# Attention block on one Trainium2 core: scores from two float32r parts, two heads in two 64-row tiles, one exponential over two banks

## The reference

```
mod = silu(c) @ wmod                       # sa, ca, ga, sb, cb, gb
h   = layernorm(x) * (1 + ca) + sa
q, k, v = lora_linear(h, ...)              # 16 heads of 16
scores  = q k^T / 4, causal mask, softmax
x   = x + ga * lora_linear(softmax(scores) v, wo, ao, bo)
h   = layernorm(x) * (1 + cb) + sb
x   = x + gb * (top-2-of-4 experts: relu(h Wi^T + lora_e) Wo^T, weighted)
```

## Time and profile before

| | |
|---|---|
| timed runs (3) | median 2151.95 us, 2151.85 to 2155.94 |
| span of the profiled execution | 2145.5 us |
| its own time | no separate one is given; the median of the runs is 6.45 us above its span |
| busy PE / DVE / ACT / POOL | 1892.0 / 1199.8 / 938.8 / 529.7 us |
| granted TensorE clock, mean | 0.959 |

### The profile page before, as it was taken

How to read it: one execution, slowest core, us unless ns; L and a number is a source line. 1 busy time by engine, 2 the same in 40 slices (tenths; PEclk the granted TensorE clock), 3 DMA queues, 4 the chain that set the end, 5 groups by cost and what they waited for, 6 DMA issues and landing times.

```text
span 2145.5 us, 36829 instructions
## 1 busy us (share of the span) xinstructions
PE 1892.0 (88%) x11124; PEld 980.5 (46%) x11124; DVE 1199.8 (56%) x2697; ACT 938.8 (44%) x1701; POOL 529.7 (25%) x823
## 2 busy tenths in 40 slices
PE   8687888999889989899889998899898998798858
PEld 5233343455435454354534555354543545344435
DVE  3755567555665557655575556655576554755132
ACT  2254444544444544544444444444445443544421
POOL 3111122322222212223223222222122232132223
PEclk9889989999999999999999999999999999999979
DMA  5523333121433222232331214332222323210100
GB/s 170 80 50 60 60 57 78 22 63 23 80 60 67 33 39 77 31 70 32 65 79 20 62 24 81 60 67 33 36 70 41 70 31 65 31 26 16 35 0 20
DMA packets 72349, 111.82 MB, mean 52 GB/s; under 512 B 13940, under 2 KB 41680, under 8 KB 72152
## 3 DMA queue, kind: packets, MB, share of 16 engines
q1 hardware_dynamic: 72136, 109.31, 27.3%
q10 hardware_dynamic: 16, 0.02, 0.0%
HBM read 75.20 MB, written 33.57 MB: 51 GB/s over the span
## 4 chain that ended last, share of the span: by engine, by line
PE 61%; DVE 14%; DMA 8%; issue 7%; SPq 5%; ACT 4%; POOL 0%; DVEq 0%; POOLq 0%; ACTq 0%
PE mxs L747 11%; PE ov L776 9%; PE st L761 9%; PE dense L856 8%; DMA k_st<-k_parts_scratch 8%; PE dense L841 5%; DVE negm L1147 4%; PE dense L867 4%; PE dense L791 4%; SPq L577 4%; PE dense L833 3%; PE dense L733 3%; PE mxs L751 2%; SPq L581 1%; DVE stats L1018 1%
## 5 line engine op out<-in xcount | busy, mean ns | idle before, releaser
L915 ACT ACTIVATE probs<-st 128x512 f32<-128x512 f32 (+1 forms) x1216 | 666.9, 576 | 651.2 <-PE st L761 613.2
L747 PE MATMUL mxs<-k_st,q_st 96*128 96x512 bf16 (+3 forms) x1536 | 463.4, 333 | 54.6 <-DMA k_st<-k_parts_scratch 48.2
L1147 DVE TENSOR_REDUCE negm<-mxs 128x1 f32<-128x512 f32 (+4 forms) x736 | 416.1, 613 | 147.8 <-PE mxs L751 147.4
L761 PE MATMUL st<-q_st,k_st 98*128 98x512 bf16 (+3 forms) x1536 | 453.0, 335 | 38.9 <-issue 24.3
L1147 DVE TENSOR_REDUCE negm_left<-mxs 128x1 f32<-128x512 f32 x512 | 330.0, 684 | 168.0 <-PE mxs L747 165.5
L776 PE MATMUL ov<-probs,v_g 128*32 128x512 f32 (+3 forms) x3072 | 333.5, 506 | 22.7 <-POOL probs L634 21.9
L747 PEld LDWEIGHTS mxs<-k_st,q_st 96*128 96x128 bf16 x1536 | 149.0, 98 | 333.9 <-issue 101.7
L856 PE MATMUL dense<-c_t,wi_t 128*128 128x512 f32 x512 | 247.3, 605 | 4.3 <-ACT ratio_b L965 3.7
L631 POOL TENSOR_TENSOR fence<-fence 128x1 f32<-128x1 f32 x256 | 49.9, 195 | 756.8 <-ACT probs L915 756.6
L761 PEld LDWEIGHTS st<-q_st,k_st 98*128 98x128 bf16 x1536 | 140.1, 99 | 202.6 <-issue 76.3
L655 POOL TENSOR_TENSOR hid<-hid,second 128x512 f32<-128x512 f32 x128 | 159.8, 1270 | 245.1 <-DVE second L1211 244.6
(11 more groups left out here) (162 smaller groups left out, 1715.3 us busy)
## 6 DMA issues: line engine op xcount, KB each, us to landing
q_st<-q_parts_scratch SPq DMA_DIRECT2D x192, 128.0 KB, 6.9
k_st<-k_parts_scratch SPq DMA_DIRECT2D x192, 128.0 KB, 7.4
q_parts_scratch<-q_part SPq DMA_DIRECT2D x16, 768.0 KB, 3.3
k_parts_scratch<-k_part SPq DMA_DIRECT2D x16, 768.0 KB, 5.4
xin<-in_L_attn_x SPq DMA_DIRECT2D x9, 1024.0 KB, 5.1
x<-in_L_attn_x SPq DMA_DIRECT2D x8, 1024.0 KB, 10.6
out_x<-ob SPq DMA_DIRECT2D x64, 128.0 KB, 1.7
q_st<-m_row SPq DMA_DIRECT2D x128, 4.0 KB
```

What stands on the lines that cost most here:

```text
L747: last = nc.tensor.matmul(mxs[:, bank_m, j * n:(j + 1) * n], q_st[0:KS, slot, h0 + j, qt * P:(qt + 1) * P], k_st[0:KS, slot, h0 + j, k0:k0 ...
L761: last = nc.tensor.matmul(st[:, score_bank(ch, kt, h0), j * n:(j + 1) * n], k_st[0:KS + 2, slot, h0 + j, kt * P:(kt + 1) * P], q_st[0:KS + ...
L915: nc.scalar.activation(probs[:, par, h0:h0 + heads, 0:n], st[:, score_bank(ch, kt, h0), 0:heads * n].rearrange("p (j q) -> p j q", q=n), A ...
L1147: nc.vector.tensor_reduce(dst[:, h0:h0 + heads], src, axis=AX.X, op=ALU.max, negate=True).then_inc(max_free, 1)
```

## The change

Queries and keys are split in two float32r parts (ACT copies the first, DVE subtracts the second; POOL's part is gone). Three products of parts replace six, so a head needs 48 rows (50 with the maximum), and two heads stand in one stack, at rows 0 and 64. The matmuls of the two heads come in pairs, in two 64-row tiles, into two banks. A `qk` step now fills both banks of `st`, and one exponential reads both; PE waits for the exponential of the step before. An `mx` step fills two of the three `mxs` banks, DVE still reduces bank by bank (42 in a group, 21 steps); the causal mask is one matmul per bank. `q_part` and `k_part` have one buffer for the two halves of the heads. The planner's costs and positions are new: each `qk` step stands at the position of the nearest `mx` step.

```diff
-Q_PARTS = (0, 0, 1, 1, 0, 2)
-K_PARTS = (0, 1, 0, 1, 2, 0)
+Q_PARTS = (0, 0, 1)
+K_PARTS = (0, 1, 0)
+SK = len(Q_PARTS) * DH
+HALF = 64
+STACK_DMAS = 2 * 2 * len(Q_PARTS)
...
+def max_banks():
+    banks = []
     for qt in range(7, -1, -1):
         if qt >= 4:
-            steps += [(h, 1, qt, 0) for h in range(HG)]
-        heads = {0: [4], 1: [2, 2] if qt < 4 else [2, 1, 1]}.get(qt % 4, [1] * HG)
-        steps += [(sum(heads[:i]), n, qt, qt // 4) for i, n in enumerate(heads)]
+            banks += [(h, 1, qt, 0) for h in range(HG)]
+        heads = 2 if qt % 4 == 0 or qt == 5 else 1
+        banks += [(h, heads, qt, qt // 4) for h in range(HG // heads)]
+def max_steps():
+    banks = max_banks()
+    return [(i, banks[i], banks[i + 1]) for i in range(0, len(banks), 2)]
...
-    heads = {128: 4, 256: 2}.get(n, 1)
-    return [("qk", slot, c, kt, h, heads) for h in range(0, HG, heads)]
+    pairs = 2 if unit_queries(c, kt)[1] <= 256 else 1
+    return [("qk", slot, c, kt, p, pairs) for p in range(0, HG // 2, pairs)]
...
-        _, _, _, heads, qt, chunk = step
-        return (max_keys(qt, chunk) + P * (qt // 4 == chunk)) * heads / 2.4
+        _, heads, qt, chunk = step[3]
+        return 200 + (max(max_keys(qt, chunk), 256) + 2 * P * (qt // 4 == chunk)) * heads / 2.4
...
-    unit_cost = [8 * 512 / 2.4 if kt < 4 * c else 8 * (512 - 128 * (kt % 4)) / 2.4 for c, kt in UNITS]
-
-    row_maxima = [0, 3, 4, 4, 5, 5, 6, 6, 6, 0, 0, 0] if post else [0, 4, 4, 5, 6, 6, 5, 5, 4, 0, 0, 0]
+    unit_cost = [500 + (2 * max(n, 256) + 4 * n) / 2.4 for n in (unit_queries(c, kt)[1] for c, kt in UNITS)]
+
+    row_maxima = [0, 2, 2, 2, 3, 3, 3, 3, 3, 0, 0, 0] if post else [0, 2, 2, 3, 3, 3, 3, 3, 2, 0, 0, 0]
...
-        turns = [((i + 0.5) / len(following), 0, s) for i, s in enumerate(following)]
-        turns += [((i + 0.35) / len(mx), 1, s) for i, s in enumerate(mx)]
+        pairs_at = [(i + 0.5) / len(mx) for i in range(len(mx))]
+        turns = [(at, 1, s) for at, s in zip(pairs_at, mx)]
+        for i, s in enumerate(following):
+            at = (i + 0.5) / len(following)
+            turns.append((min(pairs_at, key=lambda t: abs(t - at)) if mx else at, 0, s))
...
-        q_part = sb("q_part", [P, 2, 3, S], BF16)
-        q_st = sb("q_st", [P, 2, HG, S], BF16)
+        q_part = sb("q_part", [P, 2, S], F32R)
+        q_st = sb("q_st", [P, 2, HG // 2, S], F32R)
...
-                    for s in range(SPLIT):
-                        for dst, src, part in ((q_st, q_d, Q_PARTS[s]), (k_st, k_d, K_PARTS[s])):
-                            heads = src[ot, rows, part, :].rearrange("(j d) n -> d j n", j=HG)
-                            sp.dma_start(dst[s * DH:(s + 1) * DH, slot, :, :], heads).then_inc(stack_in[slot], 16)
+                    for s, (qp, kp) in enumerate(zip(Q_PARTS, K_PARTS)):
+                        for half in range(2):
+                            r0 = HALF * half + s * DH
+                            for dst, src, part in ((q_st, q_d, qp), (k_st, k_d, kp)):
+                                heads = src[ot, rows, part, :].rearrange("(p b d) n -> b d p n", p=HG // 2, b=2)
+                                sp.dma_start(dst[r0:r0 + DH, slot, :, :].bitcast(F32),
+                                             heads[half]).then_inc(stack_in[slot], 16)
...
-                elif kind == "pj":
-                    pool.wait_ge(part2_ready, done("pj") + 1)
-                    nc.gpsimd.tensor_tensor(dst[:, 2, :], rest[:, par, :], dst[:, 1, :],
-                                            ALU.subtract).then_inc(part3_ready, 1)
...
+                    after(pe, max_free, 2 * done("mx") - MAX_BANKS + 2)
                     for j in range(heads):
-                        last = nc.tensor.matmul(mxs[:, bank_m, j * n:(j + 1) * n],
-                                                q_st[0:KS, slot, h0 + j, qt * P:(qt + 1) * P],
-                                                k_st[0:KS, slot, h0 + j, k0:k0 + n], start=True, stop=True)
+                        for i in range(2):
+                            rows = slice(HALF * i, HALF * i + SK)
+                            last = nc.tensor.matmul(mxs[:, (first + i) % MAX_BANKS, j * n:(j + 1) * n],
+                                                    q_st[rows, slot, banks[i][0] // 2 + j, qt * P:(qt + 1) * P],
+                                                    k_st[rows, slot, banks[i][0] // 2 + j, k0:k0 + n],
+                                                    start=(j == 0), stop=True, skip_group_check=True)
+                            if not diagonal:
+                                last.then_inc(max_full, 1)
...
-                    after(pe, exp_done, done("qk") - SCORE_BANKS + 1)
-                    for j in range(heads):
-                        last = nc.tensor.matmul(st[:, score_bank(ch, kt, h0), j * n:(j + 1) * n],
-                                                k_st[0:KS + 2, slot, h0 + j, kt * P:(kt + 1) * P],
-                                                q_st[0:KS + 2, slot, h0 + j, q0:q0 + n], start=True, stop=True)
+                    after(pe, exp_done, done("qk"))
+                    for p in range(pairs):
+                        for i in range(2):
+                            rows = slice(HALF * i, HALF * i + SK + 2)
+                            last = nc.tensor.matmul(st[:, i, p * n:(p + 1) * n],
+                                                    k_st[rows, slot, p0 + p, kt * P:(kt + 1) * P],
+                                                    q_st[rows, slot, p0 + p, q0:q0 + n], start=True, stop=True)
...
-                    nc.scalar.activation(probs[:, par, h0:h0 + heads, 0:n],
-                                         st[:, score_bank(ch, kt, h0), 0:heads * n].rearrange("p (j q) -> p j q", q=n),
+                    heads = probs[:, par, 2 * p0:2 * (p0 + pairs), 0:n].rearrange("p (j b) q -> p b j q", b=2)
+                    nc.scalar.activation(heads, st[:, :, 0:pairs * n].rearrange("p b (j q) -> p b j q", q=n),
                                          ACT.Exp, scale=SCORE_SCALE).then_inc(exp_done, 1)
...
-                    nc.vector.tensor_tensor(rest[:, par, :], db[:, :], dst[:, 0, :],
+                    nc.vector.tensor_tensor(dst[:, 1, :], db[:, :], dst[:, 0, :].bitcast(F32),
                                             ALU.subtract).then_inc(dense_free[bank], 1)
-                    dve.wait_ge(dense_free[bank], done(f"bank{bank}") + 1)
-                    nc.vector.tensor_copy(dst[:, 1, :], rest[:, par, :]).then_inc(part2_ready, 1)
```

More of the change, by code:

```diff
@@ L26 @@
 F32 = mybir.dt.float32
+F32R = mybir.dt.float32r
 BF16 = mybir.dt.bfloat16
@@ L58 @@
 MAX_BANKS = 3
-SCORE_BANKS = 2
 NM_UNIT = NU - 3
@@ L260, in tallied @@
         names += ["scored"] * len(score_steps(*step[1:]))
-    if step[0] == "qk" and step[2] == step[3] // 4 and step[4] + step[5] == HG:
+    if step[0] == "qk" and step[2] == step[3] // 4 and step[4] + step[5] == HG // 2:
         names.append("qk diagonal")
@@ L407, in adaln_block @@
         stats = sb("stats", [P, T, 6])
-        fence = sb("fence", [P, 4])
+        fence = sb("fence", [P, 5])
         mv = sb("mv", [P, T, 2])
@@ L545, in _ @@
             sp.dma_start(bg_b[:, :], bg.partition_broadcast(P)).then_inc(ffn_in, 16)
+            sp.wait_ge(ones_ready, 1)
+            for half in range(2):
+                for slot in range(2):
+                    for p in range(HG // 2):
+                        sp.dma_start(k_st[HALF * half + SK:HALF * half + SK + 2, slot, p, :].bitcast(F32),
+                                     ones).then_inc(ones_in, 16)
             def run(step, done, it, bank):
@@ L559, in run @@
                     ot = a[0]
-                    stacked = [held(sp, done(f"rs{s}") * (2 * SPLIT * 16)) for s in range(2)]
-                    split = held(sp, done("pj"))
-                    sp.wait_ge(part3_ready, split)
+                    stacked = [held(sp, done(f"rs{s}") * (STACK_DMAS * 16)) for s in range(2)]
+                    split = [held(sp, done(f"bank{i}")) for i in range(2)]
+                    for i in range(2):
+                        after(sp, dense_free[i], split[i])
                     for s in range(2):
@@ L624, in run @@
                 if kind == "qk":
-                    slot, ch, kt, h0, heads = a
-                    if kt // 4 == ch and h0 + heads == HG:
+                    slot, ch, kt, p0, pairs = a
+                    if kt // 4 == ch and p0 + pairs == HG // 2:
                         par = UNITS.index((ch, kt)) % 2
@@ L739, in run @@
                 if kind == "mx":
-                    slot, h0, heads, qt, chunk = a
+                    slot, first, *banks = a
+                    after(pe, max_free, 2 * done("mx") - MAX_BANKS + 2)
+                    pe.wait_ge(stack_in[slot], done(f"rs{slot}") * (STACK_DMAS * 16))
+                    _, heads, qt, chunk = banks[0]
                     n = max_keys(qt, chunk)
                     k0 = chunk * HB
```

(23 more changed lines are left out.)

93 lines of the change are left out of this document (41 added, 52 removed).

## The result

| | before | after |
|---|---|---|
| median of the timed runs | 2152.48 us (2151.85 to 2155.94, 4 runs) | 2454.08 us (2438.64 to 2461.35, 4 runs) |
| ratio, 95% interval | | 1.1389 (1.1346 to 1.1432) |
| span, mean granted clock | 2145.5 us, 0.959 | 2458.7 us, 0.862 |

The change makes the kernel 13.9% slower. I had forecast 2143 us, with 2255 as the upper end: wrong in sign and outside the range.

The account below looks back on a forecast made before the run. PE's stream plus the places where it stands still was taken to bound the kernel. The terms -13 - 6 - 8 + 18 = -9 us, from 2151.95, gave 2143 us, 0.4% faster, with a range of 2050 to 2255.

Parts of the forecast that it names:

- stream term: PE's score and row-maximum matmuls as float32r pairs: between +13 and -38 us in all, middle taken, -13 us.
- DVE waits for those: Row-maximum steps queued on PE behind a waiting score step hold up DVE; mostly covered by `ov` and fillers.
- Rival 2: Single score buffer decides: score matmuls and exponential run in lockstep, +96 us in place of +18, 2221 us; chance 0.16.
- Rate: Float32r matmuls on PE stream at the bf16 rate, 0.216 us for 512 columns.
- Rival 4: Float32r streams slower than bf16 on PE: about 2360 us at two passes, above 2700 at the float32 rate; chance 0.06.
- Overlap: The two matmuls of a pair in 64-row tiles overlap, starting 0.07 to 0.11 us apart.
- rival 3: The pairs don't overlap, or each visit to the 64-row tiles costs more: +125 us, 2281 us; chance 0.12.
- Load: Each matmul of a pair needs its own 128-column load of 4-byte weights, bounded at 0.07 and 0.11 us.
- Switch: Changing PE's tiling costs 0.094 us in and out; 54 switches cost 5.1 us a group, less 1.2 beside `ov`.
- rival 1: The switch is free for 64-row tiles, or visits merge: 1993 to 2072 us, middle 2030; chance 0.16.
- The score buffer: Score banks no longer alternate, so score steps wait for the previous exponential where units are short: +18 us.
- POOL, the stacks, the exponential: Shorter PE waits: POOL before `ov` -6 us, row stacks -8 us; one exponential saves ACT 0.13 us a pair, not bound.

Follow-up runs that it names:

- e1: Kernel before with only the new steps, two-bank hand-overs, single exponential and planner, still six bf16 products in the full array: 2315.53 us, ratio 1.0778.
- e11: e4 with every row stored twice, so the stores and stack loads carry as many bytes as with float32r: 2306.55 us, ratio 1.0700.
- e6: Kernel before with only the two-bank score steps and their single exponential: 2207.71 us, ratio 1.0263.
- e5: Kernel before with only the row-maximum steps of two banks, waiting for both banks at the start, masks after both: 2307.00 us, ratio 1.0714.
- e9: e5 with each row-maximum bank waited for, filled, masked and handed to DVE before the next is touched: 2216.32 us, ratio 1.0306.
- e4: Kernel after with parts, stacks and maxima in bf16 instead of float32r, half the bytes of parts and stacks: 2206.95 us, ratio 1.0287.
- e3: Kernel after with zero rows added, 62 and 64 rows in each tile for 48 and 50: 2377.85 us, ratio 1.1044.
- e10: Kernel before with two bf16 parts and four products, third part left out, old steps and full-array mode kept: 2116.50 us, ratio 0.9843.

## Why the prediction was wrong

The steps from the kernel before to the one after, by medians, and by the ratios, which take out the difference between chips:

| step | us by medians | us by ratios | from |
|---|---|---|---|
| steps, banks and planner | +163 | +167 | 2152.5 to 2315.5, e1 |
| two tiles of 48 rows, half the products, no part for POOL, single part buffers; same bytes of the stack loads | -9 | -17 | 2315.5 to 2306.6, e11 |
| float32r in place of bf16 | +148 | +148 | 2306.6 to 2454.1 |

The profiled executions, from their pages: idle is the span less busy PE, half-clock time is worked out from the mean clock as above.

| run | span | PE busy | PE idle | half-clock time |
|---|---|---|---|---|
| before | 2145.5 | 1892.0 | 253.5 | 176 |
| e6, score steps | 2205.8 | 1916.0 | 289.8 | 243 |
| e5, `mx` steps | 2309.1 | 1952.8 | 356.3 | 291 |
| e9, `mx` bank by bank | 2213.1 | 1922.3 | 290.8 | 235 |
| e1, all steps | 2305.1 | 1935.4 | 369.7 | 267 |
| e4, bf16 tiles | 2200.0 | 1841.8 | 358.2 | 343 |
| e11, e4 with the bytes | 2316.7 | 1875.7 | 441.0 | 473 |
| e3, after with 62 rows | 2387.5 | 1993.5 | 394.0 | 463 |
| after | 2458.7 | 2070.2 | 388.5 | 679 |

The span grows by 313 us: 135 of idle PE and 178 of busy PE. Two terms that the prediction had at nothing make this up; its stream term did not fail in sum.

**The first step that failed: "DVE waits for those", at no cost.** I counted DVE's three extra reduces, found DVE not to be the bound, and left it there. But an `mx` step now takes two of three banks at once: PE's waits for DVE before `mxs` matmuls went from 4.7 to 135.3 us, nearly all of the added idle time. And in the 13 diagonal steps of the 21 it gives DVE neither bank before both are filled, since the masks come after both. That is where DVE idles: its waits grew from 147.4 to 353.7 us before the diagonal reduces (`negm`) and from 165.5 to 206.3 before the others (`negm_left`), each handed over as soon as it is filled. e5 prices the edit at +156 us, e9 gives 91 of them back by the order of fill and hand-over alone. The reduce of 684 ns, longer than the matmuls that fill its bank, made this visible beforehand: with three banks and steps of two, each step needs the first reduce of the step before to be done, where before it needed that of three steps earlier. None of my rivals had it. Rival 2 had the right shape, a lockstep for want of a buffer, at the wrong buffers.

**The second: the clock, not in the prediction at all.** I priced every matmul at 2.4 GHz. In the trace of the kernel after PE is busy in 542 us of its half-clock time, before in 126. At full clock this work would take half as long, so the clock costs 271 us for 63: +208, an estimate, and the largest part of the 313. In e1, which has the new steps without the tiles, it is 95 us, so only some 32 come with the waits of the steps. e3 shows one cause: the same instructions over 62 and 64 rows for 48 and 50 raise the mean from 0.862 to 0.903 and take 76 us off. Why e11 gains only 9 us on e1, where the stream should give 125, is the clock in part (0.898 for 0.942, 473 against 267 us of half-clock time) and idle time in part (441.0 for 369.7 us).

**The stream: about right in sum, by luck.** *Rate*: the engine streams float32r at the bf16 rate: a pair of 512 columns behind another pair takes 0.33 us with the switch, where bf16 in e4 takes 0.31. Rival 4 is out. *Overlap*: the two matmuls of a pair start 3 ns apart (median of the pairs in the trace), not 0.07 to 0.11, and the pair costs the columns of one, so the first half of rival 3 is out as well. *Load*: this failed. I let the load set the pace of a pair's second matmul, which was too dear, and had no load at the entry of a visit, which was too cheap. In float32r the first pair of a visit to the 64-row tiles costs 0.12 us over its columns, the pairs behind it 0.01 to 0.02 (at 256 columns and more). So the same two matmuls of 256 columns take 0.21 us behind another pair and 0.32 alone, both with the switch to the full array:

```profile
910.68 0.44 PE L760 MATMUL st<-q_st,k_st 50*128 50x384 f32 x2
910.96 0.28 PE L739 MATMUL mxs<-k_st,q_st 48*128 48x256 f32 x2
911.17 0.29 PE L748 MATMUL mxs<-causal_b,ident_b 128*128 128x128 bf16 x2
...
913.17 0.38 PE L739 MATMUL mxs<-k_st,q_st 48*128 48x256 f32 x2
913.49 0.28 PE L748 MATMUL mxs<-causal_b,ident_b 128*128 128x128 bf16 x2
```

The second half of rival 3, "each visit costs more", thus came true in part. The weight loads fit this. First of the kernel after, then of e4, those of a first pair and of the pair behind it:

```profile
904.27 0.19 PEld L760 LDWEIGHTS st<-q_st,k_st 50*128 50x128 f32 x2 [0.33 <-issue]
904.38 0.19 PEld L739 LDWEIGHTS mxs<-k_st,q_st 48*128 48x128 f32 x2
```

```profile
912.93 0.10 PEld L762 LDWEIGHTS st<-q_st,k_st 50*128 50x128 bf16 x2 [0.64 <-issue]
912.94 0.10 PEld L741 LDWEIGHTS mxs<-k_st,q_st 48*128 48x128 bf16 x2
```

In both, the first pair's loads start with its matmuls, the next pair's while the first still streams. A float32r load lasts 0.19 us for 0.10, and the next can start only 0.11 later for 0.01. I read the 0.12 us as the part of the first load that nothing covers; no run changed the load alone. The Trainium skill ("TensorE: Matmul & The Clock Gate", Weight-path perf modes) says that the fast weight load needs 128 weights and an input type other than FP32. The trace agrees and puts float32r with FP32: 0.19 against 0.10 us for the same shape, and the plain float32 loads of 128 columns for L867 of the kernel before average 192 ns. *Switch*: 0.31 us from a 512-column bf16 pair to the full array is 0.094 over its columns, as forecast; rival 1 is out. (Where the prediction says that without the drain the sum would be the second rival, it means this one, the first.)

With the measured terms a group has 7.9 us of columns, 27 visits x 0.11 = 3.0 of uncovered loads and 3.9 of switches: 14.8 against the 15.7 removed, -29 us in 32 groups where I had -13. Without the loads it would be 11.8, or -125. The difference, some 95 us, is stream at full clock; the step from e11 to the kernel after was measured as 148, with 52.5 us less idle time. PE's work at half clock went from 345 to 542 us, which by the estimate above costs 98 us more. So float32r costs about as much by the clock that falls with it as by its loads; what links the two is not shown.

**The score buffer: right mechanism, wrong size.** Forecast +18, measured +57 in e6. PE's wait for the exponential before score matmuls grew from 3.4 to 31.2 us there (19.3 in the kernel after), its idle time by 36 in all. Its busy time grew by 24 with as many matmuls, and its half-clock time from 176 to 243 us: again the clock, which I had not priced.

**POOL, the stacks, the exponential.** PE's wait for POOL before `ov` fell from 21.9 to 1.5 us, 20 where I had 6, but not for my reason. In e6, where POOL still does all its subtractions, the new score steps alone bring it to 2.6 us; in e10, without the subtractions and with the old steps, it is 9.9. The wait for the stacks fell from 48.2 to 45.0, 3 for 8. One exponential over 1024 takes 1024 ns, two of 512 took 1194; ACT's 49 us less were not on the path, as forecast.

**What stays open.** Why the clock falls with fewer rows beyond that it does, and why it falls with float32r and with the bytes; which of the 42 reduces and the new places makes the 65 us that e9 keeps; why e5 and e6 together are less than their sum. The planner's new costs and places were not run alone. A version with the bank-by-bank hand-over of e9 in bf16 tiles with 62 rows was not tried.

## What to carry to other kernels

When a step is changed to use several buffers at once, price the hand-over before the arithmetic: count the buffers, set the consumer's time for one against the producer's, and see whether the consumer gets the first one before the last is written. Row tiles are worth their stream only if the visits to them are long enough to pay for entry and exit (here 0.094 us each way, and with float32r 0.11 of uncovered load at the entry), and if the clock holds. Take the load's duration for the very type from a trace, and if none has it, let the range reach to its being uncovered once a visit. Change the structure and the number format in separate steps: here the old structure with fewer bf16 parts gained 1.6%, and each half of the change lost: the steps 163 us, the float32r tiles 139 more.

## What the runs showed of the hardware

- The granted clock depended on the rows of a matmul, zeros included: 62 rows for 48 in two 64-row tiles raised it from 0.862 to 0.903 (float32r) and from 0.922 to 0.945 (bf16), 76 and 37 us.
- A float32r matmul streams at the bf16 rate, but its weight load takes 0.19 us for 0.10 at full clock, and the first pair of each visit to 64-row tiles takes 0.11 us more than in bf16 (0.34 for 0.23 at 512 columns). Behind another pair it is 0.33 for 0.31, with the switch.
- The two matmuls of a pair in two 64-row tiles start 3 ns apart and cost the columns of one.
- Loads of 128 KB into 16 rows, issued twelve at a time, land in 7.0 us, of 64 KB in 2.8: more than twice as long. Doubling the bytes of these loads and of the stores before them cost the kernel 100 us.
- Useless matmuls put in to keep TensorE busy cost 227 us for 145 us of columns, in part because they broke up visits to the tiles, and left the half-clock time where it was, 681 against 679 us.
